# Cross attention over a long context: values computed per tile, and one matmul per head with high and low parts side by side

## The reference, cut to what matters

```
x = x + xattn(layernorm(x), ctx_1024, ...)     # x 128 x 256, context 12544 x 256
x = x + attn(layernorm(x), ...)                # self attention, 16 heads of 16, LoRA
x = x + ffn(layernorm(x), ...)                 # fp8 linear 256 -> 256

def xattn(latents, context, ln_l_w, ln_l_b, ln_c_w, ln_c_b, Wq, Wkv, Wo, bo):
    lat = layernorm(latents, ln_l_w, ln_l_b)
    ctx = layernorm(context, ln_c_w, ln_c_b)
    q = lat @ Wq                               # 16 heads of 64
    k, v = split(ctx @ Wkv)                    # 12544 keys and values
    attn = softmax(clip(q k^T / 8, -11, 11))   # per head 128 x 12544
    return (attn @ v) @ Wo + bo
```

## Time and profile before

| | |
|---|---|
| median of 3 runs | 1160.64 us (1160.17 to 1162.14) |
| the profiled execution | 1157.79 us |
| its span, first to last instruction | 1156.1 us |
| mean granted TensorE clock | 0.986 |
| busy: PE, PEld, DVE, ACT, POOL | 98%, 81%, 72%, 52%, 27% |

### The profile page before, as it was taken

The page is one execution under the profiler, slowest core; times in us unless marked ns, Lnnn a source line. Parts: engine busy times, 40 slices in busy tenths (PEclk is TensorE's granted clock), DMA queues, the critical chain, the costliest instruction groups (busy, mean ns, idle before and its releaser), DMA issues.

```text
span 1156.1 us, 18331 instructions
## 1 busy us (share of the span) xinstructions
PE 1137.3 (98%) x5056; PEld 936.4 (81%) x5056; DVE 829.5 (72%) x1622; ACT 598.8 (52%) x1029; POOL 309.0 (27%) x516
## 2 busy tenths in 40 slices
PE   6999999999999999999999999999999999999997
PEld 5888888888888888888888888888888888888774
DVE  5778778777777777787776776776766766766624
ACT  4555555555555555555555555555555555555411
POOL 5334334334334233242221221221211211211100
PEclk8999999999999999999999999999999999999996
DMA  5221221221211211354212212212112112110000
GB/s 178 69 69 46 68 68 45 68 63 51 68 61 53 68 55 59 108 108 81 74 46 69 67 46 68 62 51 68 57 56 68 53 61 68 51 64 24 1 1 5
DMA packets 81393, 70.72 MB, mean 61 GB/s; under 512 B 40115, under 2 KB 67670, under 8 KB 81366
## 3 DMA queue, kind: packets, MB, share of 16 engines
q1 hardware_dynamic: 80390, 68.94, 20.1%
q10 hardware_dynamic: 976, 1.45, 0.4%
HBM read 70.13 MB, written 0.13 MB: 61 GB/s over the span
## 4 chain that ended last, share of the span: by engine, by line
PE 96%; issue 2%; DMA 1%; DVE 1%; POOL 0%; ACT 0%; SPq 0%; POOLq 0%; DVEq 0%; ACTq 0%
PE bank L466 31%; PE bank L467 31%; PE bank L468 31%; PE bank L511 1%; DMA wkT<-in_WkT_dram 1%; PE bank L572 1%; PE bank L584 1%; PE bank L503 0%; PE bank L614 0%; PE bank L596 0%; PE bank L630 0%; PE bank L594 0%; POOL wkT L457 0%; DVE fold_y L909 0%; PE bank L604 0%
## 5 line engine op out<-in xcount | busy, mean ns | idle before, releaser
L732 ACT ACTIVATE ex<-bank,c_rstd 128x512 f32<-128x512 f32 x392 | 270.1, 689 | 242.4 <-PE bank L468 166.4
L403 POOL TENSOR_TENSOR z_lo<-z,z_hi 128x255 fp32r<-128x255 f32 x196 | 174.9, 892 | 742.1 <-ACT z_hi L745 742.1
L739 ACT CAST p_hi<-ex 128x512 fp32r<-128x512 f32 x392 | 243.8, 622 | 240.8 <-DVE ex L899 148.6
L903 DVE TENSOR_TENSOR p_lo<-ex,p_hi 128x512 fp32r<-128x512 f32 x392 | 271.6, 693 | 116.3 <-ACT p_hi L739 99.7
L466 PE MATMUL bank<-qk_hi,d_hi 128*128 128x512 f32 x784 | 305.9, 390 | 0.0
L467 PE MATMUL bank<-qk_lo,d_hi 128*128 128x512 f32 x784 | 305.5, 390 | 0.0
L466 PE MATMUL bank<-p_hi,z_hi 128*128 128x512 f32 x784 | 305.5, 390 | 0.0
L468 PE MATMUL bank<-p_hi,z_lo 128*128 128x512 f32 x784 | 305.5, 390 | 0.0
L468 PE MATMUL bank<-qk_hi,d_lo 128*128 128x512 f32 x784 | 305.3, 389 | 0.0
L467 PE MATMUL bank<-p_lo,z_hi 128*128 128x512 f32 x784 | 305.2, 389 | 0.0
L899 DVE TENSOR_SCALAR ex<-ex 128x512 f32<-128x512 f32 x392 | 189.8, 484 | 156.5 <-ACT ex L732 154.6
(11 more groups left out here) (162 smaller groups left out, 410.0 us busy)
## 6 DMA issues: line engine op xcount, KB each, us to landing
t_all<-in_ctxT_dram SPq DMA_DIRECT2D x98, 384.0 KB, 3.2
x_pair<-in_ctx_dram SPq DMA_DIRECT2D x98, 256.0 KB, 2.7
diff<-sig_all SPq DMA_DIRECT2D x194, 0.5 KB, 1.9
wq<-in_Wq_dram ACTq DMA_DIRECT2D x2, 512.0 KB, 6.9
wkT<-in_WkT_dram SPq DMA_DIRECT2D x2, 512.0 KB, 6.1
wv<-in_Wv_dram SPq DMA_DIRECT2D x1, 1024.0 KB
wo<-in_Wo_dram SPq DMA_DIRECT2D x1, 1024.0 KB
crow_all<-in_crows_dram ACTq DMA_DIRECT2D x1, 256.0 KB, 7.6
```

Source lines behind the costliest of these rows:

```text
L403: pool.tensor_tensor(z_lo[s][:, b, 0:LAST], z[s][:, b, 0:LAST], z_hi[s][:, b, 0:LAST].bitcast(F32), ALU.subtract).then_inc(s_zlo, 1)
L732: act.activation(ex[c][:, :], sc_bank[c][:, :], ACT.Exp, scale=c_rstd[s4][:, b:b + 1])\
L739: act.copy(p_hi[b][c][:, :], ex[c][:, :]).then_inc(s_phi, 1)
L903: dve.tensor_tensor(p_lo[b][c][:, :], ex[c][:, :], p_hi[b][c][:, :].bitcast(F32), ALU.subtract)\
```

## The change

- **Values per tile.** Wv is folded with the norm's weights (`value_fold`) ahead of the passes, and split (`wv_hi`, `wv_lo`). `values` multiplies the tile's centred columns with it: 128 keys by 512 columns (8 heads of 64), 6 matmuls into one bank `v_bank`. ScalarE scales it by rstd into the high part (`v_high`), VectorE makes the low part (`v_low`). z, z_hi and z_lo go, and so does the load of rows in pass 1.
- **One matmul per head.** The weights are [v_hi, v_lo] of a head (128 columns), what moves is [p_hi, p_lo] (2 x 128 columns). The four products land in different places and are added later: over the columns by `save`, over the partitions by the projection, with Wo laid twice.
- **Denominators.** VectorE adds the clipped probabilities of every tile into `den` (`add_den`). A product with ones gives the sum over keys, which is inverted and multiplied with the outputs (`inverse`, `normalised`), for pass 0 inside pass 1, for pass 1 after it.
- **Moved.** `difference` goes from VectorE to GpSimd, behind a wait for `s_dlo`; `d_hi` from VectorE to ScalarE. Wk is folded by TensorE (`key_fold`) and no more by VectorE. The preparation of pass 1 lies in pairs 41 to 44 of pass 0, after each half. The projection of pass 0 lies in pass 1. Weights come in halves, Wo in pass 1.
- exp(g+1, c) waits for add_den(g, c), no longer for p_lo(g, c). values(g+1) waits for v_low(g).

The diff, cut to its core:

```diff
@@ gpsimd
             def pair(p, i, phase):
...
+                pool.wait_ge(s_tin[s3_4], landed(p, i, phase, 3, SLOTS))
+                pool.wait_ge(s_dlo, gp + 2)
+                difference(s3_4, s3)
+                if not (static and p == 0 and i == 0):
+                    pool.wait_ge(s_exp, 2 * CH * gp)
+                    pool.wait_ge(s_vlo, 2 * gp)
+                if p == 0 and not over:
+                    ctx_rstd(gp + 3, s3, s3_4, i + 3)
+                else:
+                    ctx_again(s3_4, i + 3 - PAIRS if over else i + 3)
@@ tensor
+            def values(p, gp, s, b, first=False):
...
+                if not first:
+                    pe.wait_ge(s_vlo, g)
+                keys, cols = slice(b * P, (b + 1) * P), slice(p * IH, (p + 1) * IH)
+                for k in range(KD):
+                    ins = mm3(v_bank[:, :], d_hi[s][:, k, keys], d_lo[s][:, k, keys], wv_hi[:, k, cols], wv_lo[:, k, cols],
+                              k == 0, k == KD - 1)
+                ins.then_inc(s_v, 1)
...
+            def weighted_sum(gp, b, c, start, stop, saved=0):
...
+                for m in CHUNK_M[c]:
+                    for a in range(2):
+                        at = a * CM + m % CM
+                        ins = pe.matmul(acc[m][:, a, :, :], vhl[b][:, 2 * m + a, :, :].rearrange("p n d -> p (n d)"),
+                                        ph[b][c][:, :, at * P:(at + 1) * P], start=start and a == 0,
+                                        stop=stop and a == 1)
+                ins.then_inc(s_pv, 1)
...
+                    if not ended:
+                        values(next_p, gp + b, slot(p, phase, b, 2), 1 - b)
                     for c in range(CH):
                         if not ended:
                             scores(next_p, gp + b, slot(p, phase, b, 2), 1 - b, c)
-                        weighted_sum(gp, slot(p, phase, 0, 2), b, c, first, last, saved=p * KD if first else 0)
+                        weighted_sum(gp, b, c, first, last, saved=p * CM if first else 0)
@@ scalar
+                    if more1:
+                        v_high(g + 1, s4, 1 - b, used=not (begun and b == 0))
                     for c in range(CH):
                         if more1:
+                            exps(g + 1, s4, 1 - b, c)
+                            p_high(g + 1, 1 - b, c, used=not (begun and b == 0))
+                        if (b, c) == (1, 0) and not (ended and i + 2 >= PAIRS):
...
+                            act.copy(d_hi[s2][:, :, :], diff[s2][:, :, :]).then_inc(s_dhi, 1)
@@ vector
+            def v_low(g, s4, b):
+                dve.wait_ge(s_vhi, g + 1)
+                dve.scalar_tensor_tensor(vhl[b][:, :, 1, :], v_bank[:, :].rearrange("p (h d) -> p h d", h=HP),
+                                         c_rstd[s4][:, b:b + 1], vhl[b][:, :, 0, :].bitcast(F32), ALU.mult, ALU.subtract)\
+                   .then_inc(s_vlo, 1)
...
+            def add_den(p, g, c, first=False):
...
+                    dve.tensor_tensor(den[p][c], den[p][c], ex[c][:, :], ALU.add).then_inc(s_den[c], 1)
...
+                    if more1:
+                        clip(g + 1, 0)
+                        if b == 1:
                             dve.wait_ge(s_crstd, stored(p, i, 1))
+                        v_low(g + 1, s4, 1 - b)
+                        p_low(g + 1, 1 - b, 0)
+                    if b == 0 and new_stats:
+                        ctx_stats(gp + 3, landed(p, i, phase, 3, SLOTS), s3_4, 0)
+                    if over and b == 1:
+                        save(p, 0)
+                    if more1:
+                        clip(g + 1, 1)
+                    if b == 0 and new_stats:
+                        ctx_stats(gp + 3, landed(p, i, phase, 3, SLOTS), s3_4, 1)
+                    if more1:
+                        add_den(next_p, g + 1, 0, first=next_p > p)
+                    if b == 1 and not (ended and i + 2 >= PAIRS):
+                        d_low(gp + 2, slot(p, phase, 2, 2))
...
+                    if more1:
+                        p_low(g + 1, 1 - b, 1)
+                    if b == 0 and new_stats:
+                        ctx_aggr(s3, 0)
+                        ctx_aggr(s3, 1)
+                    if more1:
+                        add_den(next_p, g + 1, 1, first=next_p > p)
...
+                    if p == 1 and extra in DEN_STEPS:
+                        inverse(extra, side_bank)
+                        normalised(0, extra)
...
+            def save(p, c):
+                dve.wait_ge(s_pv, CH * (TILES * (p + 1) - 1) + c + 1)
+                for m in CHUNK_M[c]:
+                    dve.tensor_reduce(osum[p][c][:, :, m % CM, :], acc[m].rearrange("p a n q -> p a q n"), AX_X, ALU.add)\
+                       .then_inc(s_save[c], 1)
+
+            def inverse(n, src):
+                dve.wait_ge(s_denp, n + 1)
+                dve.reciprocal(rden[n % CH][:, :], src[:, :]).then_inc(s_rden, 1)
...
```

More of the change, by code:

```diff
@@ L52, in perceiver_layer @@
     HT = P // AD
[L53 to L55 removed]
+    assert N == P and D == 2 * P and ctx.shape[1:] == (P, 2, D)
     with ExitStack() as stack:
@@ L358, in pair @@
                         late(dst, src)
+                if static and p == 1 and i == 0:
+                    sp.wait_ge(s_wkEp, 2 * PASSES)
+                    sp.wait_ge(s_wvp, KD * PASSES)
+                    for half in range(2):
+                        sp.dma_start(wo2[half * DH:(half + 1) * DH, :, :], Wo).then_inc(s_wo, 16)
             assert (PAIRS - LOOPED - 1) * 3 >= len(late_loads)
@@ L537, in _ @@
                 scores(0, 0, 0, 0, c, first=True)
+            pe.wait_ge(s_wv[0], 16)
+            for k in range(KD):
+                value_fold(0, k, bank[k])
+            pe.wait_ge(s_wq[1], 16)
+            q_heads(1, range(MH), side_bank)
+            pe.wait_ge(s_wvlo, KD)
+            values(0, 0, 0, 0, first=True)
+            pe.wait_ge(s_qT, CH + 1)
             def pair(p, i, phase):
@@ L788, in pair @@
                         if more1:
-                            exps(g + 1, slot(p, phase, b, SLOTS), 1 - b, c)
-                            p_high(g + 1, 1 - b, c, used=not (start and b == 0))
-                        if c != b and not ended:
-                            z_high(gp + 1, slot(p, phase, 1, 2), b, used=not start)
-                if static and p == 0 and i in FOLD_PAIRS:
-                    centre(MH + FOLD_PAIRS.index(i))
-                if static and p == 0 and i in QK_PAIRS:
-                    for a in range(CH):
-                        qk_high(KD * CH + CH * QK_PAIRS.index(i) + a, 1, QK_PAIRS.index(i), a, bank[6 + a])
@@ L964, in pair @@
                 static = isinstance(i, int)
-                start = static and p == 0 and i == 0
                 ended = static and p == PASSES - 1
-                more = [not (ended and i + n >= PAIRS) for n in range(4)]
+                over = static and i == PAIRS - 1
                 new_stats = p == 0 and not (static and i + 3 >= PAIRS)
@@ L1037, in save_chunk1 @@
-            def save_chunk1(p):
-                dve.wait_ge(s_pv, CH * TILES * (p + 1))
-                for k in range(KD):
-                    dve.tensor_copy(sums[:, k, p * HP * P + CW:(p + 1) * HP * P], acc[k][1][:, :])\
-                       .then_inc(s_save[1], 1)
-            passes(dve, pair)
-            dve.memset(wvE[:, 0, :, DH:VW], 0.0)
-            dve.tensor_copy(wvE[:, 1, :, DH:VW], last_row[:, 0:1].unsqueeze(1).to_broadcast([P, H, 1])).then_inc(s_wvden, 1)
-            save_chunk1(PASSES - 1)
+                    more1 = not (ended and over and b == 1)
@@ L1051, in fp8_weights @@
+            for c in range(CH):
+                if c:
+                    save(1, c)
+                inverse(CH + c, DEN_BANK[c])
+                normalised(1, c)
             def fp8_weights():
```

722 lines of the change are left out of this document (353 added, 369 removed).

## The result

The changed kernel takes 1180.43 us (median of 4 runs, 1178.63 to 1184.1), the kernel before 1161.39 us beside it. The ratio is 1.0168, with a 95% interval of 1.0138 to 1.0199: 19 us slower, where the prediction had 10 us slower. The profiled execution is the longest of the four, 1184.1 us.

The account below looks back on a forecast made before the run. TensorE (98% busy) bounds the kernel before; after the change, VectorE's waits and GpSimd's collision hold pairs above TensorE's 10.11 us. 1157.8 + 4 (loop) + 5 + 12 (extras) - 9 (tail) = 1170, stated as 1171 us; own range 1150 to 1195.

Parts of the forecast that it names:

- The collision: Half b=1: GpSimd's difference stops VectorE's add_den, taking 1.08 us per pair; next clip at 6.12 instead of 5.04.
- second limit: One value bank: values wait for the previous tile's v_low; 4.74 us clip to clip, replacing pass 1's 4.05.
- TensorE's pair: TensorE's own work per pair of tiles in the loop: 10.11 us against 10.87 before, with 256-column matmuls at 0.121 us.
- rival 3: 256-column matmuls cost 0.228 us, a pair 11.82 on TensorE, about 1257 us; chance 0.10 together with other stalls beyond 1195.
- One of the signs that the prediction named: Pairs of 10.8 to 11.0 us in the passes, those with statistics (pass 0) longer.
- steady loop: Pairs of 10.97 us in pass 0 and 10.86 in pass 1 against 10.87: loop 4 us longer.
- start, to the first clip of the pairs: Ahead of the pairs: folds and values added on TensorE, folding on VectorE gone; taken as 0, between -4 and +4.
- extras, both passes: Work added inside the passes: +5 us in pass 0's pairs 41 to 44, +12 in pass 1.
- tail, from the last tile's first clip: After the loop: 12.4 us instead of 19.4 to the cross attention, and 2 off after it; together -9 us.
- the reciprocals: VectorE's 512-column reciprocals of denominators, in pass 1 and the tail: 3.2 us each, from a line through small ones.
- Rival 1: TensorE binds: GpSimd's difference finds a gap, everything hidden under 10.11 us a pair; 1092 us, chance 0.20.
- Rival 2: The collision costs half: pairs of 10.4 and 10.3 us, 1118 us; chance 0.20.

Follow-up runs that it names:

- experiment 1: Changed kernel with GpSimd's difference inside the pairs cut to 8 of 256 columns of each half: 1103.5 us, ratio 0.951 to the kernel before.
- experiment 3: Changed kernel with the difference back on VectorE in half b=1, between the first p_low and the second clip: 1101.4 us, ratio 0.950.
- experiment 5: Changed kernel with each second tile's v_low issued one step earlier, ahead of the last add_den of half b=1: 1139.8 us, ratio 0.984.
- experiment 4: Changed kernel with v_low on half its columns (4 of the 8 heads): 1163.4 us, ratio 1.0025.
- experiment 6: Changed kernel with each of the four reciprocals of denominators on 64 of 512 columns: 1167.7 us.
- experiment 2: Changed kernel with the difference back on VectorE in half b=0, ahead of the second clip: 1113.65 us, ratio 0.960.

## Where the prediction went wrong, and what of it held

**In short.** The prediction had the loop 4 us longer and the kernel 10 us slower; the loop got 16 longer and the kernel 19 slower. The collision that it put first is there at the size that it gave. The term that failed is its "second limit", the way through the one value bank, sized at 4.74 us and measured at 4.91.

**The mechanism held.** TensorE's pair fell as worked out: 10.11 predicted, 10.16 once nothing stood in its way (experiments 1 and 3), and 256 columns took 0.12 us for 0.121, so rival 3 is out. The collision was sized right, half b=1 at 6.12 predicted and 6.14 to 6.15 measured. GpSimd's difference starts 4.00 us after the first clip of half b=1 (about 4.0 predicted), and the add_den over 1.5 us stands where it was looked for. It ends 0.55 us behind GpSimd's difference, as predicted. The clip of 0.97 us in the earlier trace rows, which the prediction laid to GpSimd without its row, did stand beside GpSimd's z_lo (200.83 to 201.56 us). Experiment 1 shows that this one instruction decides the sign. The Trainium skill (GPSIMD Engine Reference, section Key points) has GpSimd contend with VectorE's instructions of two SBUF inputs or in a 2-port mode. The traces agree as far as they go: add_den and d_lo (two inputs in SBUF) took 1.78 us, and v_low, with an input in PSUM, kept its 0.75 in experiment 5. A clip (one input) took 1.40; that it runs in a 2-port mode is not shown, only that alone it takes 0.43 us where instructions of two inputs take 0.69.

**The step that failed: the way through the one value bank.** It was sized at 4.74 us, below the 4.85 of VectorE's order in pass 0, and so bound only in pass 1. It is 4.91 and binds in both. In pass 0 VectorE's order alone would have allowed 4.80 (experiment 4). One of the signs that the prediction named did not appear for this reason: pairs with statistics should have been longer, and both passes have 11.06. Term by term, from the rows above against the earlier trace rows: clip to v_low 0.34 (0.35), v_low 0.74 (0.69), start of the values 0.05 (0.05), the twelve matmuls to the last one's start 2.63 (2.50), last matmul to exp 0.43 (0.42), exp to clip 0.72 (0.73).

Most of the miss, 0.13 of 0.17 us, is in the matmuls: the first is followed by the second after 0.34 us (806.29 - 805.95) and not after 0.227, as it came out of a wait. That holds for all 63 matmuls of 512 columns that came out of a wait from 150 to 450 and from 600 to 1000 us, at 0.33 or 0.34 us each. The term thus was priced by rows of a TensorE that never waits. The trace of before has such a place too, at the end of pass 1, and it shows the same 0.34 us:

```profile
1093.21 0.50 PE L466 MATMUL bank<-p_hi,z_hi 128*128 128x512 f32 x1
...
1093.55 0.39 PE L467 MATMUL bank<-p_lo,z_hi 128*128 128x512 f32 x1
```

The likely reason is the load of its weights, which starts with it (PEld at 805.95) and in the stream lies under the matmul before; that was not tested. The rest of the miss, 0.05, is v_low. The prediction took the price of L919, which also has an input in PSUM; L961 scales as well and takes 0.742, but that the scaling is the cause was not tested either.

With it the steady loop grows by 98 x 0.185 = 18 us, less 2 for the last two pairs, which have no difference to make and take 10.17 and 10.15; that is 16 where 4 was predicted. Experiments 4 and 5 show that this way sets half b=0: with v_low 0.27 us shorter the half of pass 1 is 0.27 shorter, and with v_low moved ahead it falls to 4.20. Of the sum, 49 x 0.17 us in pass 1 and 49 x 0.06 in pass 0 are 11 of the 12 us missed in the loop.

**A second cause, on which both limits stand.** The prediction added the two halves; it did not ask whether v_low could go elsewhere. It sits behind a clip that the collision has delayed, starting at 805.16, though ScalarE had its input ready at 802.71:

```profile
802.03 0.68 ACT L802 ACTIVATE vhl<-wide,c_rstd 128x512 fp32r<-128x512 f32 x1
```

In that sense the value bank's limit was a matter of order, and worth some 40 us.

**The other terms**, from the profiled execution (span 1182.4 against 1156.1, +26.3; it was the longest of its four runs, and the one of before, 1157.8 us, lies under its median, so the sum lies above the medians' 19):

| term | predicted | measured |
|---|---|---|
| start, to the first clip of the pairs | 0 | +1.1 |
| steady loop | +4 | +16 |
| extras, both passes | +17 | +17 |
| tail, from the last tile's first clip | -9 | -7.8 |
| sum | +12 | +26.3 |

Among the extras the reciprocals took 3.35 us for 3.2, in pass 1 and tail alike. Here the Trainium skill (VectorE: DVE Perf Modes, section First, the fixed hardware budget) gives a repeat count of 8, an estimated 4.3 us; the measured 3346 ns for 512 columns, and (3346 - 548)/448 = 6.2 ns a column between 64 and 512, decide for the line drawn through two small reciprocals.

That the tail's -7.8 is so near to -9 is partly luck. It holds 2.1 us that the last tile of the loop became shorter, which the prediction had not put there. The tail to the cross attention went from 19.4 to 14.3 us, not to 12.4, and from there to the end only 0.7 us were won, not 2. Part of the reason is the granted clock by these reciprocals: 0.76 over the 25 us from 1120, where experiment 6 has 1.00 at the same place of its tail. This differs between executions: the stretch from the last tile's first clip to the end took 59.6 us here and in experiment 1, but 55.6 and 56.0 in experiments 3 and 2, with the same instructions.

The changed kernel, then experiment 6:

```profile
1120.00:1145.00 25.00, 20.55 (x74) 13.86 (x73) 19.56 (x29) 4.52 (x7) 0.55 (x1) 0.76 0.00 1
...
1111.00:1136.00 25.00, 22.36 (x103) 15.23 (x101) 18.11 (x36) 6.56 (x12) 2.45 (x2) 1.00 0.00 1
```

**Rivals.** Rival 1 (TensorE binds) is what experiments 1 and 3 make of the kernel; it was priced at 1092 and is 1101. 98 x 0.05 us are 5 of the 9. The extras are the rest and more: in experiment 3's profile the pairs that carry them are 23 us longer than before's beyond the steady difference, where the rival had 15, while the tail is 11.9 shorter, where it had 9. Rival 3's 1257 starts from 1157.8 us, the other two from 1160.6; from there it would be 1260. Rival 2 (half of the collision) fell at once: half b=1 shows all of it.

## What to carry to other kernels

Work handed to an idle engine is not free if it shares a path to memory with the engine that binds: here 0.69 us of VectorE's became 1.1 us of standing still, at the one place where the next tile waited. Before moving an operation off a busy engine, look for a wait in that engine's own order that can hold it; here the wait for p_hi did, and the kernel went from 1180 to 1101 us. And price a loop that is to wait by rows taken behind a wait: the first matmul cost 0.11 us more there than in a stream.

## What the runs showed of the hardware that I had not expected

- A matmul of 512 columns that comes out of a wait is followed by the next after 0.33 to 0.34 us (63 of 63), not 0.22 to 0.24.
- GpSimd gets in between two instructions of VectorE that are issued back to back, and then the whole of VectorE's next one waits: the stretch is not a slower rate but a stop (1.78 us = 1.23 to the end of GpSimd's instruction and 0.55 of its own). The prediction had this from one place of the trace before; it holds behind three instructions in a row too. A one-input clip is stopped too (1.40 us = 1.11 and 0.29 of its own), and v_low with its input in PSUM is not.
- The granted clock was 0.91 over the 30 us in which TensorE stood idle for 6.3 us, and 1.00 in the steady loop, where it stands idle for 6% (from 600 to 1000, 22.7 of 400 us):

```profile
600.00:1000.00 400.00, 377.28 (x1883) 315.40 (x1882) 348.09 (x542) 244.05 (x399) 81.04 (x72) 1.00 0.13 36
```
